# Where a tile's row numbers for its scatter are copied, and how an expert's weight cast is shared by two engines

## What is computed

```
scores = jax.nn.softmax(x @ gate_w.T, axis=-1)
topk_w, topk_ids = lax.top_k(scores, TOP_K)
topk_w = topk_w / (topk_w.sum(-1, keepdims=True) + 1e-20)
def _swiglu(x, w13_, w2_):
    gu = x @ w13_.T
    g, u = jnp.split(gu, 2, axis=-1)
    return jax.nn.silu(g) * u @ w2_.T
...
    y = _swiglu(x, w13_e, w2_e)
    return (acc + c_e[:, None] * y, None)
out, _ = lax.scan(body, jnp.zeros_like(x), (w13, w2, combine.T))
out = out + _swiglu(x, sw13, sw2)
```

## Time and profile before

| what | value |
|---|---|
| median of 3 runs | 1419.17 us (1418.41 to 1422.58) |
| the profiled execution: its own time | 1422.3 us |
| its span, first to last instruction | 1420.5 us |
| TensorE matmuls busy | 1307.5 us, 92% |
| VectorE busy | 851.5 us, 60% |
| ScalarE busy | 729.5 us, 51% |
| GpSimd busy | 944.7 us, 67% |

### The profile page before, as it was taken

The page is one execution under the profiler, slowest core; times in us unless marked ns, Lnnn a source line. Parts: engine busy times, 40 slices in busy tenths (PEclk is TensorE's granted clock), DMA queues, the critical chain, the costliest instruction groups (busy, mean ns, idle before and its releaser), DMA issues.

```text
span 1420.5 us, 31069 instructions
## 1 busy us (share of the span) xinstructions
PE 1307.5 (92%) x8064; PEld 1175.1 (83%) x8065; DVE 851.5 (60%) x1570; ACT 729.5 (51%) x1317; POOL 944.7 (67%) x671
## 2 busy tenths in 40 slices
PE   7897998998988899999789999999999999999995
PEld 2676887887888789999678988888988898888895
DVE  5879888897989865653244444444444445444441
ACT  5898887988879554343233333333333333333331
POOL 0589898999888847888366556666556665556722
PEclk8899999998999999999999999999999999999999
DMA  4121122223242555655487878887878778877752
GB/s 138 34 73 38 54 68 97 68 68 97 69 130 61 145 142 105 141 100 129 92 246 209 213 185 214 219 213 210 216 181 220 214 199 221 210 191 212 203 134 37
DMA packets 136276, 205.91 MB, mean 145 GB/s; under 512 B 20496, under 2 KB 74384, under 8 KB 134016
## 3 DMA queue, kind: packets, MB, share of 16 engines
q1 hardware_dynamic: 101744, 102.33, 23.8%
q0 software_dynamic: 31024, 62.10, 23.6%
q10 hardware_dynamic: 3440, 40.63, 8.1%
HBM read 130.99 MB, written 76.25 MB: 146 GB/s over the span
## 4 chain that ended last, share of the span: by engine, by line
PE 33%; POOL 12%; issue 9%; DMA 8%; DVE 4%; ACT 2%; POOLq 1%; ACTq 1%; DVEq 0%
PE bank L1814 11%; PE bank L1794 9%; PE bank L1795 9%; DMA out_x<-ys,aid 7%; POOL token_lists L1086 6%; POOL w L1046 4%; PE bank L1805 2%; POOL out_x L1068 1%; DVE hs L1236 1%; ACT w L876 1%; PE bank L1704 1%; PE bank L1690 1%; DVE xl L1439 1%; DMA out_x<-ys 1%; POOLq L1091 1%
## 5 line engine op out<-in xcount | busy, mean ns | idle before, releaser
L1794 PE MATMUL bank<-w,xh 128*128 (+1 forms) x1088 | 365.3, 337 | 26.0 <-DVE xl L1439 24.5
L1008 POOL TENSOR_TENSOR hc<-hs,crow 128x512 f32<-128x512 f32 x254 | 322.1, 1302 | 91.8 <-DVE hs L1236 86.2
L1795 PE MATMUL bank<-w,xh 128*128 (+1 forms) x1088 | 351.3, 323 | 0.0
L1074 POOL DMA_INDIRECT out_x<-ys,aid x104 | 165.2, 1589 | 254.6 <-issue 226.4
L1236 DVE TENSOR_TENSOR_SCAN hs<-dA,bank 128x512 f32<-128x512 f32 x256 | 295.7, 1208 | 50.3 <-PE bank L1704 31.6
L1814 PE MATMUL bank<-w,ah 128*128 (+1 forms) x816 | 259.3, 399 | 15.3 <-DVE al L1485 15.3
L1485 DVE TENSOR_TENSOR al<-bank,ah 128x384 fp32r<-128x384 f32 x136 | 75.8, 558 | 294.9 <-ACT ah L921 279.7
L1794 PEld LDWEIGHTS bank<-w,xh 128*128 128x128 f32 x1088 | 204.7, 188 | 42.5 <-issue 34.3
L927 ACT COPY ys<-bank 128x512 f32<-128x512 f32 x136 | 79.9, 587 | 262.8 <-PE bank L1814 262.8
L1795 PEld LDWEIGHTS bank<-w,xh 128*128 128x128 f32 x1088 | 206.7, 190 | 4.5
L1814 PEld LDWEIGHTS bank<-w,ah 128*128 128x128 f32 x816 | 150.2, 189 | 44.0 <-issue 12.9
(11 more groups left out here) (184 smaller groups left out, 1983.6 us busy)
## 6 DMA issues: line engine op xcount, KB each, us to landing
raws<-in_wall ACTq DMA_DIRECT2D x16, 2176.0 KB, 8.9
token_quarters<-xt SPq DMA_DIRECT2D x104, 256.0 KB
xs<-token_quarters SPq DMA_DIRECT2D x104, 256.0 KB, 3.2
crow<-c_rows SPq DMA_DIRECT2D x64, 256.0 KB, 3.3
xt<-token_rows_turned SPq DMA_DIRECT2D x32, 256.0 KB, 2.9
out_x<-ys POOLq DMA_DIRECT2D x32, 256.0 KB, 4.2
token_rows<-rowb SPq DMA_DIRECT2D x4, 1028.0 KB, 5.9
xrow<-in_x SPq DMA_DIRECT2D x4, 1024.0 KB, 8.0
```

The lines of the kernel that those rows point to most:

```text
L1008: nc.gpsimd.tensor_tensor(hc[:, j, :], hs[:, j, :], crow[:, n % 4, :], ALU.mult).then_inc(hc_done, 1)
L1074: pool.indirect_dma_start(out_rows, bass.IndirectOffsetOnAxis(ap=aid[:, s:s + 1], axis=0), ys[:, s, :], None, bounds_check=TOKENS - 1, oob ...
L1794: nc.tensor.matmul(gate_bank[:, 0:I], xx, columns(w, off + ww + k * 2 * I, I), start=first, stop=last)
L1795: mm = nc.tensor.matmul(up_bank[:, 0:I], xx, columns(w, off + ww + k * 2 * I + I, I), start=first, stop=last)
```

## The change

It does two things. `add_ids` moves: in VectorE's tile t it copied the row numbers of tile t+1 ahead of `gather_ids` and xl(t+1), behind a wait for the scatter of t-3; now it copies those of tile t behind `multiply` of t, behind a wait for the scatter of t-4. The last tile gets a copy of its own. And `SHARE` goes from 2176 to 3264 columns, so that ScalarE casts 1088 columns of a set and VectorE 3264.

```
-SHARE = WCOLS // 2
+SHARE = 3 * WCOLS // 4
...
                 if takes and not plain:
                     take_weight(t + TAKEN, slot_of(TAKEN), number, group_of(TAKEN))
                     keep_ids(t + TAKEN, slot_of(TAKEN))
-                if not static or t + 1 >= NS:
-                    add_ids(t + 1, slot_of(1))
                 if static and t < NS:
                     for late in FIRST_ROWS.get(t, ()):
...
                     gather_ids(t + AHEAD, slot_of(AHEAD), column)
                 x_low(t + 1, 1 - s)
                 multiply(t, place % 4)
+                if not static or t >= NS:
+                    add_ids(t, place % 4)
                 if not static or t >= PEELED:
                     next_weights(t, split)
...
             multiply(last, 3)
+            add_ids(last, 3)
             a_low(last, 1)
```

## The result

The changed kernel takes **1383.3 us** (median of 4 runs, 1380.75 to 1383.9) against 1419.14 for the kernel before (4 runs): a ratio of **0.974** with a 95% interval of 0.9725 to 0.9757. The forecast was 1385, in a range of 1380 to 1397. On another chip a second set of 4 runs gave 1385.98 (1384.45 to 1387.21) against 1420.68, a ratio of 0.9753 [0.9737, 0.977].

A forecast was written before the change was run, and what follows sets the result against it. TensorE's matmuls bound the routed stage, with 34.9 us of holes; less 0.5 left over, 34.4 off the profiled 1422.3 gives 1387.9, or 1384.8 as median: forecast 1385, own range 1381 to 1389, 8 in 10 range 1380 to 1397.

The forecast's parts named there:

- The bound: Routed stage: bound by TensorE's own matmuls, 6.29 us from one tile's ys copy to the next, with holes between.
- the sum of the holes: Routed stage: 676.49 us for 102 ticks against 641.6 undisturbed, so 34.9 us of holes, of which 34.4 go.
- The move: VectorE's aid copy, behind multiply: its wait for a scatter costs nothing and the whole xl hole is saved.
- The cover: New waiting place: scatter of cast tile S lands 4.8 us early; TensorE feels it only 7.1 us later than now.
- the link: Expert start: if VectorE's cast blocks GpSimd's scatter of the tile before the cast, 0.65 us later; otherwise nothing; 1385 either way.
- The casts: Expert start: VectorE's cast takes 1.94 us (bounds 1.87 and 1.94), ScalarE's 1.09; VectorE becomes the later one.
- left over at al: TensorE's wait for al at expert starts: 0 to 0.13 us per expert, 0 to 2.0 in all, taken as 0.5.
- the rival that another transfer is late: At xl, a later tile's gather or transposition replaces the wait; only al's 10 to 11 us won: 1409, chance 0.05.
- the split of the sum: Per expert start: 0.76 us late at al plus 1.43 at xl, 15 times, 32.9 of the 34.9 us.
- third rival: At xl, a later tile's gather or transposition is late instead; only al's 10 to 11 us won: 1409, chance 0.05.
- The first rival: VectorE's longer cast and new wait leave al as late as now; only xl's part is gained: 1395, chance 0.11.
- The slower rival: A scatter outlasts the new place, holding al and the down matmuls; at 16 us 24 us slower, 1443; chance 0.05.

The follow-up runs named there:

- the cast alone: Kernel before with only VectorE's share of the weight cast raised from half to three quarters, aid copy in its old place: 1430.42 us, ratio 1.0066.
- the move alone: Changed kernel with the cast share put back to half on each engine, so only the aid copy moves: 1395.41 us, ratio 0.9821.
- doubled subtraction: Changed kernel with GpSimd's weight subtraction done twice at each expert start: 1461.94 us, ratio 1.0292; the same edit on the kernel before: 1590.71 us, ratio 1.1199.

## Why the prediction was right, and where its steps were off

- **The bound, and the sum of the holes.** Right: of 34.9 us 34.4 were to go, 33.6 went, and the tick of 6.29 is what is left. One figure of the range has no working: its low end takes off 35.4 us, more than all the holes; with 34.9 it would be 1381.5, which changes nothing here.
- **The move.** Right, 24.4 us by itself. The cover was there as worked out: 9.8 us of delay cost VectorE 5.49 (a slack of 4.3, forecast 4.8, or 4.2 with the link) and TensorE 3.07 (6.7, forecast 7.1) in the start shown; on the mean of the starts the slack was 4.5 and 6.5.
- **The casts.** VectorE's was taken at 1.94 and measured 1.860; the low bound, with the fixed part of a small copy (1.87), came closest. ScalarE's 1.107 met the 1.09 by slope. So VectorE's cast and transposition end at 883.28, 2.50 after the cast's start, earlier than the 2.67 or 2.87 of the prediction; in the start shown al waits 0.28 for ah instead, so ScalarE still holds al, where the prediction expected VectorE to. Neither is late for TensorE: of the up to 2.0 us that could be left over at al nothing is. Of the 1.3 us of holes that remain, 0.84 is one event in the third routed tile: a transposition waited 4.6 us for a transfer (the waits above), and al behind it. In the second trace of the same kernel the transposition waits 3.9 us in the same place, but TensorE doesn't wait for al and the stage is 642.2. That is all that shows in the changed kernel of the rival that another transfer is late: one event at the start of the stage, and none for xl.
- **The link between cast and scatter.** The rows of before left open whether there is one; the casts of four lengths show that there is, but only where they overlap. The scatter of S-1 mostly starts 1.40 to 1.45 us after the cast, however long that is, and ends at about 3.01 with casts of 0.73 and 1.29, at 3.32 with 1.86 and at 3.60 with 2.15, some 1.46 after the cast's end in the last two. In the changed kernel that is 0.31 us, not the 0 or 0.65 that the prediction put against each other: before, the cast ended 0.12 ahead of the scatter and so held nothing. TensorE doesn't feel it there; in the cast alone it is the 0.25 per start by which the chain grows. The Trainium skill, "SBUF — State Buffer", section "Who interferes with whom", has whichever of the two issues second blocked until the first is done, for a VectorE copy that uses two ports. No run here shows the ports, but these rows agree with such a block but for 0.13 us: fully blocked from 1.42 on, the scatter would end at 1.86 + 1.59 = 3.45, where it ended at 3.32.
- **The step that was off: the split of the sum.** The prediction added 0.76 at al and 1.43 at xl per start, and built its third rival on al's 10 to 11 us being won alone (1409). No run shows al's part won alone: without the move the share wins nothing (1430.4 and 1422.7 for three quarters and one quarter). A later gather or transposition holding xl with the move made, as that rival has it, was not run. The hole at xl was the difference between GpSimd's chain of 19.4 us and TensorE's work in that time, so a shorter hole at al made it longer by as much. The total was right only because both parts are made together: the move takes the chain off the path, and from then on al's hole is worth its 9.2 us (652.1 less 642.9; 9.9 by the second trace's 642.2). The first rival, which leaves the al hole, is the move alone to half a us (1395, measured 1395.4).
- **The slower rival's price** was too low in kind: it counted only what the wait outlasts. The doubled subtraction shows a hole of 3.07 us that costs 4.87.

It stays open why the clock fell after some holes and not after others. In the cast alone TensorE waited for xl 1.05 to 2.62 us at the fifteen starts; the clock fell after those of 2.62, 1.75 and 1.90, and not after those of 2.34, 2.33 and 2.17, so the length of the hole alone doesn't decide it. With the doubled subtraction it fell after 2.73 and 3.74 us and not after 3.19, 3.33 and 3.50. No run varied that by itself.

## What to carry to other kernels

Before two holes of a period are added up, measure from a common start to the end of each: if one engine's chain sets the date of the later hole, the earlier one lies in its shadow and is worth nothing until that chain is off the path. So take the wait away first, by an older slot or a place behind the work that TensorE needs next, and balance the load after it. Of two changes that belong together, one can look useless or even harmful alone: here the share, 0.7% slower without the move and some 9 us of gain with it.

## What was not expected of the hardware

- A VectorE cast in SBUF stretched GpSimd's issue of a scatter that began inside it: 1.59 us without overlap, 1.87 to 1.93 beside a cast of 1.86 us, 2.15 to 2.21 beside one of 2.15, where it began some 1.4 us after the cast. In the one start where it began 1.75 us after the cast it took 1.59 and 1.86.
- A wait of TensorE could cost more than its length: after waits of 1.75 and 3.07 us the granted clock was down by what 3.4 us at 1.2 GHz make, some 1.7 us more, while the holes of up to 1.5 us in the kernel before left it at 1.00.
